# A graph kernel's count matrix laid out in DRAM with four rows of a partition side by side

## The reference

```
x_t = mlp2(x, W1n, b1n, W2n, b2n);  e_t = mlp2(edge_attr, W1e, b1e, W2e, b2e)
out = x + segment_sum(x_t[src] * e_t * dp_scale, dst) * res_w
x   = layernorm(x + layernorm(out) * gamma + beta)      # layer 1, then its norm
row, col = [src, loops], [dst, loops];  deg = segment_sum(1, col)
for _ in range(2):                                      # two hops
    h = segment_sum(deg^-1/2[row] * deg^-1/2[col] * h[col], row)
x   = layernorm(x + (h @ W.T + b))
```

## Time and profile before

| what | us |
|---|---|
| timed, median of 3 runs | 7476.43 (7473.94 to 7482.64) |
| profiled execution, its span | 9194.2 |
| own time of the profiled execution | none is given beside its span |
| stage of the profile: setup, to the first edge MLP | 0 to 180 |
| phase 1 | 180 to 6890 |
| norm | 6890 to 7001 |
| the two hops | 7001 to 9168 |
| tail | 9168 to 9194 |

### The profile page before, as it was taken

How to read it: one execution, slowest core, us unless ns; L and a number is a source line. 1 busy time by engine, 2 the same in 40 slices (tenths; PEclk the granted TensorE clock), 3 DMA queues, 4 the chain that set the end, 5 groups by cost and what they waited for, 6 DMA issues and landing times.

```text
span 9194.2 us, 153579 instructions
## 1 busy us (share of the span) xinstructions
PE 6574.3 (72%) x51112; PEld 5130.6 (56%) x51113; DVE 4933.3 (54%) x6884; ACT 4449.3 (48%) x6632; POOL 3623.7 (39%) x3315
## 2 busy tenths in 40 slices
PE   6566666666666666666666565666565899999999
PEld 3344444444444444444444444444344899989998
DVE  2455555555555555555555555555557455545555
ACT  1344444444444444444444333344333677766666
POOL 1565555655555565565444444444430000010000
PEclk9666666666666666666666666666667999999999
DMA  3233333333333333333232222223223566666665
GB/s 105 49 60 59 64 54 65 64 55 64 55 63 55 64 58 61 64 59 57 45 53 51 51 52 50 52 48 51 49 47 115 175 200 193 200 180 187 191 189 168
DMA packets 1979721, 809.87 MB, mean 88 GB/s; under 512 B 1680075, under 2 KB 1906563, under 8 KB 1978995
## 3 DMA queue, kind: packets, MB, share of 16 engines
q1 hardware_dynamic: 1845056, 677.46, 32.6%
q0 software_dynamic: 107552, 121.32, 6.2%
q10 hardware_dynamic: 27018, 9.90, 0.4%
HBM read 590.00 MB, written 218.34 MB: 88 GB/s over the span
## 4 chain that ended last, share of the span: by engine, by line
PE 50%; issue 16%; another core or an unknown queue 13%; ACT 10%; DVE 8%; DMA 1%; DVEq 1%; ACTq 1%; POOL 0%; SPq 0%; POOLq 0%
PE compared L869 11%; PE bank L944 11%; ACT arena L670 7%; PE bank L856 6%; PE compared L944 5%; PE bank L837 4%; PE sums L425 3%; PE sums L944 3%; DVE U L1215 2%; PE bank L850 2%; DVE arena L388 1%; DMA arena<-counts 1%; ACT H L661 1%; PE bank L860 1%
## 5 line engine op out<-in xcount | busy, mean ns | idle before, releaser
L573 POOL DMA_INDIRECT arena<-node_rows,arena x3125 | 3448.8, 1104 | 3205.4 <-DVE bank L1176 2112.9
L670 ACT ACTIVATE arena<-compared 98x512 uint8<-98x512 f32 x3936 | 2201.2, 597 | 2141.2 <-PE compared L869 1355.0
L869 PE MATMUL compared<-U 128*128 128x128 bf16 x15744 | 1861.4, 267 | 1718.1 <-issue 868.7
L869 PEld LDWEIGHTS compared<-U 128*128 128x128 bf16 x15744 | 1196.2, 117 | 2379.9 <-ACT arena L670 1137.2
L738 ACT ACTIVATE arena<-arena 128x1792 bf16<-128x1792 uint8 x868 | 1470.1, 1697 | 706.3 <-DMA arena<-counts 354.3
L1215 DVE TENSOR_TENSOR U<-iota_share,arena 128x1568 bf16<-128x1568 bf16 x984 | 958.6, 974 | 1075.8 <-PE compared L869 987.4
L1305 DVE CAST arena<-arena 128x1792 bf16<-128x1792 uint8 x868 | 948.5, 1094 | 1042.9 <-PE sums L944 587.0
L944 PE MATMUL bank<-arena 128*128 (+1 forms) x13440 | 1391.3, 247 | 9.4 <-issue 9.3
L1215 DVE TENSOR_TENSOR U<-iota_b,arena 128x2048 bf16<-128x2048 bf16 x984 | 1194.0, 1213 | 0.0
L944 PEld LDWEIGHTS bank<-arena 128*128 128x128 bf16 x13440 | 1138.2, 98 | 13.6 <-issue 13.0
L944 PE MATMUL compared<-arena 128*128 (+1 forms) x6720 | 1107.0, 247 | 34.1 <-DMA arena<-hop_parts,first_dst 23.5
(11 more groups left out here) (199 smaller groups left out, 4493.0 us busy)
## 6 DMA issues: line engine op xcount, KB each, us to landing
arena<-counts SPq DMA_DIRECT2D x1736, 224.0 KB
counts<-arena SPq DMA_DIRECT2D x124, 1568.0 KB, 7.2
arena<-in_edge_attr SPq DMA_DIRECT2D x125, 448.0 KB
arena<-node_rows,arena POOLq DMA_INDIRECT x3125
hop_parts<-arena ACTq DMA_DIRECT2D x14, 672.0 KB, 4.6
arena<-in_x_t SPq DMA_DIRECT2D x13, 256.0 KB, 2.6
node_rows<-H SPq DMA_DIRECT2D x1, 3136.0 KB, 16.4
edge_rows<-arena SPq DMA_DIRECT2D x1, 3125.0 KB
```

The lines of the kernel that those rows point to most:

```text
L573: e.indirect_dma_start(out=rows[:, q, k, :], out_offset=None, in_=node_rows, in_offset=bass.IndirectOffsetOnAxis(ap=src_i[:, t:t + 1], axi ...
L670: nc.scalar.activation(stage[0:B, k, v:v + VB, :].rearrange("p v n -> p (v n)"), compared[0:B, c % 2, :], ACT.Copy).then_inc(s_ev, 1)
L869: mm = nc.tensor.matmul(compared[:, c % 2, n * P:(n + 1) * P], HOH[:, j % 2, VB * c + n, :], LOH[:, j % 2, VB * c + n, :], start=True, sto ...
```

## The change

The count matrix keeps its values and its bytes. What moves is the place of each in DRAM, and with it the order in which the hop takes them.

- **Layout.** `counts` was [124·128 rows, 12,544 columns]; it is now [124·32, 98·512]. Rows 4v to 4v+3 of a block stand side by side for each node block, so that a store writes 3,136 pieces of 512 bytes in place of 12,544 of 128.
- **Hop loads.** A DRAM row now holds four count rows, and 128 DRAM rows are a whole round. A load takes all four row blocks for some of the range's 14 node blocks: `BS` = 4, 3, 4 and 3 of them. The buffers of DVE (a = 0, 2) have 2,048 bytes per partition, those of ACT (a = 1, 3) 1,536; all had 1,792.
- **Hop matmuls.** `hop_block` runs four matmuls in a row into the same half bank, one for each row block; before, successive matmuls went to successive halves. The first and last rounds go by buffer, with the same 14 zero matmuls.
- **Which row is which.** The rows of the partitions are permuted, so the tables are too: POOL makes a selection table `pick` (a memset and an affine_select of 128 by 2,048), PE applies it with 16 float32 matmuls of 62 columns behind a new wait (`s_hop_rows`), and DVE copies the two tables out of PSUM behind another (`s_picked`). Two small memsets go.
- **Gathers.** The tiles' first targets take 26 tile columns (`TC`) in place of 25, the last four of 96 rows, and their load is three DMAs, not two. Each hop has 26 gathers. The zero block's hop rows need no memset now (L1277), and the waits for the last stores stay.

```diff
+    PIECE = RING * P
+    BS = [(0, 4), (4, 7), (7, 11), (11, 14)]
-        counts = nc.dram_tensor("counts", [RB * P, COLS], u8).ap()
+        counts = nc.dram_tensor("counts", [RB * PR, B * PIECE], u8).ap()
...
             def store_block(k, q):
                 e.wait_ge(s_ev, last_use(k) + (1 + 2))
-                e.dma_start(counts[bass.ds(k * P, P), :].rearrange("v (a b) -> a v b", b=P), stage[0:B, q, :, :])\
-                    .then_inc(s_cst[q], 16)
+                e.dma_start(counts[bass.ds(k * PR, PR), :].rearrange("v (a c) -> a v c", c=PIECE),
+                            stage[0:B, q, :, :].rearrange("a (v w) n -> a v (w n)", w=RING)).then_inc(s_cst[q], 16)
...
-                        e.dma_start(raw[:, a, :, :].rearrange("p b n -> p (b n)"),
-                                    counts[bass.ds((n * RING + a) * P, P), ig * BG * P:(ig + 1) * BG * P])\
+                        b0, b1 = BS[a]
+                        row0 = (n + (a + 1)) * P - (a + 1) * P
+                        e.dma_start(raw[a], counts[bass.ds(row0, P), (ig * BG + b0) * PIECE:(ig * BG + b1) * PIECE])\
...
+            e.memset(pick, 0.0).then_inc(s_fill, 1)
...
+            e.affine_select(out=pick, in_=pick, compare_op=ALU.not_equal, fill=1.0,
+                            base=0, pattern=[[P, RING], [-1, RING], [1, P]], channel_multiplier=-RING)
...
-                for s in range(TB):
+                for s in range(TC):
...
-                        nc.scalar.activation(ring[:, a, :, :], raw[:, a, :, :], ACT.Copy).then_inc(s_conv[a], 1)
+                        nc.scalar.activation(ring[a], raw[a], ACT.Copy).then_inc(s_conv[a], 1)
...
+            e.wait_ge(s_hop_rows, 1)
+            for k in range(RING):
+                for w in range(RING):
+                    mm = nc.tensor.matmul(
+                        picked[:, k, :, :], pick[:, k, w, :],
+                        row_table[:, :, :].rearrange("p a (r w) -> p a r w", w=RING)[:, :, :, w:w + 1]
+                        .rearrange("p a r w -> p a (r w)"), start=(w == 0), stop=(w == RING - 1))
+            mm.then_inc(s_picked, 1)
...
+            def hop_block(h, ig, n, a, rows_of):
+                e.wait_ge(s_conv[a], n + (rounds_before(h, ig) + 2))
+                b0, b1 = BS[a]
+                for b in range(b0, b1):
+                    o = hop_bank[b // 2][:, b % 2 * 3 * D:(b % 2 + 1) * 3 * D]
+                    for w in range(RING):
+                        at_b = (b - b0) * PIECE + w * P
+                        mm = nc.tensor.matmul(o, ring[a][:, at_b:at_b + P], rows_of[w], start=False, stop=False)
+                mm.then_inc(s_afree[a], 1)
...
             def last_round(h, ig):
                 n = ROUNDS - 1
-                for a in (0, 1):
-                    hop_block(h, ig, n, a, hop_in[h][:, n * RING + a, :])
-                bank_by_bank(h, ig, n, (2, 3), last=True)
+                rows_of = [moving(h, n, w) for w in range(RING)]
+                for a in range(RING):
+                    hop_block(h, ig, n, a, rows_of)
+                    for j in range(BS[a][0] // 2, BS[a][1] // 2):
+                        nc.tensor.matmul(hop_bank[j][:, 0:6 * D], ones_b[0:1, :], zeros_b[:, 0:6 * D],
+                                         start=False, stop=True).then_inc(s_bank, 1)
...
-            link(nc.vector.memset(row_dst[:, FULL:RB], -1.0))
-            link(nc.vector.memset(row_tile_f[:, FULL:RB], 0.0))
...
+            e.wait_ge(s_picked, 1)
+            nc.vector.tensor_copy(row_dst[:, :].rearrange("p (r k) -> p k r", k=RING), picked[:, :, 0, :])
+            nc.vector.tensor_copy(row_tile[:, :].rearrange("p (r k) -> p k r", k=RING), picked[:, :, 1, :])\
+                .then_inc(s_rows_made, 1)
...
-            for h in range(2):
-                if h == 1:
-                    for q in range(2):
-                        e.wait_ge(s_cst[q], 16 * ((FULL + 1 - q) // 2 + 1))
-                nc.vector.memset(hop_in[h][:, FULL:RB, :], 0.0).then_inc(s_empty, 1)
+            for q in range(2):
+                e.wait_ge(s_cst[q], 16 * ((FULL + 1 - q) // 2 + 1))
...
-                nc.vector.tensor_copy(ring[:, a, :, :], raw[:, a, :, :]).then_inc(s_conv[a], 1)
+                nc.vector.tensor_copy(ring[a], raw[a]).then_inc(s_conv[a], 1)
```

More of the change, by code:

```diff
@@ L41, in gnn_two_layers @@
     COLS = B * P
+    PR = P // RING
+    LAST = P - PR
+    TC = RB - B
+    TW = TC - RING
+    assert RB == FULL + 1 and TW * P + RING * LAST >= T > TW * P + (RING - 1) * LAST
     IG = 7
@@ L44, in gnn_two_layers @@
     ROUNDS = RB // RING
-    assert RB == FULL + 1 == G - 1 and BG * IG == B and BG % 2 == 0 and BG // 2 == 7
+    assert RB == G - 1 and BG * IG == B and BG % 2 == 0 and BG // 2 == 7
     V = 16
@@ L918, in _, with moving @@
             sum_by_node(e, regs, G - 1, 0, 0, parts_2[:, 0])
-            def bank_by_bank(h, ig, n, of, first=False, last=False):
-                for a in of:
-                    e.wait_ge(s_conv[a], n + (rounds_before(h, ig) + 2))
+            def moving(h, n, w):
+                if isinstance(n, int):
+                    return hop_in[h][:, n * RING + w, :]
+                return hop_in[h][:, bass.ds(n * RING + w, 1), :].rearrange("p a f -> p (a f)")
+            def hop_block(h, ig, n, a, rows_of):
[7 more added lines that the diff above has]
+                mm.then_inc(s_afree[a], 1)
@@ L924, in bank_by_bank, with first_round @@
+            def first_round(h, ig):
                 before_it = banks_before(h, ig)
-                for j, o in enumerate(hop_bank):
-                    if first:
+                rows_of = [moving(h, 0, w) for w in range(RING)]
+                for a in range(RING):
+                    for j in range(-(-BS[a][0] // 2), -(-BS[a][1] // 2)):
                         if before_it:
                             e.wait_ge(s_taken, before_it - len(hop_bank) + j + 1)
-                        nc.tensor.matmul(o[:, 0:6 * D], ones_b[0:1, :], zeros_b[:, 0:6 * D], start=True, stop=False)
-                    for a in of:
-                        for i in range(2):
-                            mm = nc.tensor.matmul(o[:, i * 3 * D:(i + 1) * 3 * D], ring[:, a, 2 * j + i, :],
-                                                  hop_in[h][:, n * RING + a, :], start=False, stop=False)
-                        if j == len(hop_bank) - 1:
-                            mm.then_inc(s_afree[a], 1)
-                    if last:
-                        nc.tensor.matmul(o[:, 0:6 * D], ones_b[0:1, :], zeros_b[:, 0:6 * D], start=False, stop=True)\
-                            .then_inc(s_bank, 1)
@@ L940, in hop_block @@
-            def hop_block(h, ig, n, a, moving):
-                e.wait_ge(s_conv[a], n + (rounds_before(h, ig) + 2))
-                for b in range(BG):
-                    o = hop_bank[b // 2][:, b % 2 * 3 * D:(b % 2 + 1) * 3 * D]
-                    mm = nc.tensor.matmul(o, ring[:, a, b, :], moving, start=False, stop=False)
-                mm.then_inc(s_afree[a], 1)
-            def first_round(h, ig):
-                bank_by_bank(h, ig, 0, (0, 1), first=True)
-                for a in (2, 3):
-                    hop_block(h, ig, 0, a, hop_in[h][:, a, :])
+                        nc.tensor.matmul(hop_bank[j][:, 0:6 * D], ones_b[0:1, :], zeros_b[:, 0:6 * D],
+                                         start=True, stop=False)
@@ L958, in hop @@
             def hop(h, ig, first, last):
                 with e.Fori(first, last) as n:
+                    rows_of = [moving(h, n, w) for w in range(RING)]
                     for a in range(RING):
-                        hop_block(h, ig, n, a, hop_in[h][:, bass.ds(n * RING + a, 1), :].rearrange("p a f -> p (a f)"))
+                        hop_block(h, ig, n, a, rows_of)
             def first_hop_sweep(h):
```

65 lines of the change are left out of this document (40 added, 25 removed).

## The result

The changed kernel takes **7461.0 us** (median of 8 runs, 7454.8 to 7463.1) against 7476.65 for the kernel before (8 runs, 7473.9 to 7482.6): a ratio of 0.9976, 95% interval [0.9967, 0.9985], 15.6 us faster. The forecast was 7,482 us with "no change" as the likeliest case. The time lies inside the range, but a small gain that is clear of the noise was not what I forecast.

What follows compares the result with a forecast made beforehand. The prediction held phase 1 bound by POOL and PE side by side and the hops by PE alone. Small terms (2 + 0.6 − 1 − 0.3 + 2.8 + 1.3) summed to +5.4 us, giving 7,482 us, range 7,345 to 7,575.

Steps and rivals of the forecast that it cites:

- Between column ranges: Where one column range of the hops follows another: 14 zero matmuls cost 0.38 us each, nothing is late, 0.
- The store, 0 on the path: Count-block store in phase 1: 8 us or less in 512-byte pieces, but no engine waits for it, so 0.
- Four matmuls in a row into a region, 0: PE in the hops: four successive matmuls adding into the same region cost nothing extra, 0.
- rival C: Hops, slower: adding four times in a row into one region costs 2.1 ns, +51 us, so 7,533; chance 0.12.
- Conversions: Hops: DVE's conversion goes from 1.094 to 1.25 us, ACT's from 1.697 to 1.45.
- DVE being late, +2: Hops: a guessed six late loads cost DVE's longer conversions about 0.3 us more each, +2 us, bounds 0 and 95.
- Gathers, +2.8: POOL in the hops: one more gather per hop, awaited by each hop's first range, 2 × 1.39 = +2.8 us.
- Setup +1.3: Setup: 16 float32 matmuls with waits and copies take 8.6 us, mostly covered; 1.3 us charged (0 to 8.6).
- Start of the hops −1: Start of the hop: PE's first matmul needs only DVE's buffer 0, ready about 1 us earlier, −1 (0 to −1.5).
- Phase 1 is bound by POOL and PE side by side: Phase 1, timed group of 40.3 us: POOL needs 36.6 us, PE is busy 34.8, so both bind it.
- A: Phase 1, faster: timed groups wait for stores; 7,359 if one us per store counts, floor 7,023; chance 0.29.
- B: Hops, slower: DVE's buffers come late, 0.33 us at each of 289 waits for a load, +95 us, 7,577; chance 0.14.

Runs made afterwards that it cites:

- e2: The changed kernel with its zero matmuls one by one again, each next to its bank's own matmuls: 7477.75 us, ratio 0.9999 to the kernel before.
- e3: The changed kernel with the 128-byte store of the kernel before: 7461.8 us, ratio 0.9980 to the kernel before.
- e5: The kernel before with only its store changed, to 512-byte pieces: 7478.4 us, ratio 0.9999 to the kernel before.
- e9: The changed kernel without the setup's 16 float32 matmuls and their wait, tables copied unpermuted: 7461.2 us, ratio 0.9978 to the kernel before.
- e12: The changed kernel with zero matmuls of 128 contracted rows in both the hops and phase 1: 7437.1 us, ratio 0.9945 to the kernel before.
- e10: The changed kernel with the hops' zero matmuls contracting 128 rows in place of one: 7435.6 us, ratio 0.9949 to the kernel before.
- second profile: The kernel before, unchanged, profiled once more in one execution: 7480.0 us, profiled span 7478.2 us.

## Why the prediction was wrong

**The step that failed** is "Between column ranges": "each of 14 zero matmuls costs 0.38. [...] Nothing is late, 0." The 0.38 was a mean, and I carried it over as if it were a price of the matmul. It is 0.16 for the matmul and 0.21 for each switch out of and back into the real ones, and the change, by walking buffers in place of banks, cuts the switches from 13 to 7. Worth 13 × 1.3 = −17 us, measured −17.5 alone and +16.7 undone. The rows that show it were there to be read in the first trace as in the second: from a zero matmul to the next zero one 0.17 us (5639.23 to 5639.40), to the next real one 0.27 (5635.02 to 5635.29). From the first trace:

```profile
7338.24 0.33 PE L937 MATMUL compared<-zeros_b,ones_b 1*128 1x384 bf16 x1
7338.50 0.51 PE L932 MATMUL sums<-arena 128*128 128x192 bf16 x4
7338.94 0.33 PE L937 MATMUL sums<-zeros_b,ones_b 1*128 1x384 bf16 x1
7339.11 0.32 PE L929 MATMUL compared<-zeros_b,ones_b 1*128 1x384 bf16 x1
```

**The other terms.** Their sum was +5.4 and is 0.0 (e2 against before). One by one:

- The store, 0 on the path: right. Undone it costs 0.7 us (e3), done alone 0.6 (e5), both within the noise. Its own time was right too (8 us or less; it is 7).
- Four matmuls in a row into a region, 0: right. The ranges of e2 take 148.2 us, as the shortest ones of before; rival C, 2.1 ns each, would have shown as +3.6 us per range.
- Conversions, 1.25 and 1.45 us forecast: 1.227 and 1.483 measured. DVE being late, +2: it is +4.9 (waits of PE for L1305 or L1334 in range 0: 3.6 us before, 8.5 after), but ACT's greater slack, to which I gave no price, takes back 1.5 there (1.94 to 0.45) and 3.5 up to the last range, where PE waited 4.24 us for ACT and 0.22 for DVE before, and now 0.95 for DVE alone.
- Gathers, +2.8 for two hops: only hop 0 pays. Its wait for the gathered rows grew from 24.35 to 28.0 us, +3.65, more than the one instruction of 1.39, as POOL's mean rose from 1178 to 1302 ns in this pair. (Over all profiles the wait is 23.5 to 25.5 us with 25 gathers and 26.0 to 28.2 with 26.) Hop 1 has no such wait.
- Setup +1.3: 0 (e9). Start of the hops −1: the wait ahead of the first zero matmul is 2.7 us shorter, since it no longer waits for ACT's first conversion, which began after DVE's. The first real one comes 1.8 earlier: from the start of DVE's first conversion to it are 3.11 us before (5298.93 to 5302.04) and 1.28 after (5293.48 to 5294.76).
- "Phase 1 is bound by POOL and PE side by side": not so for PE's busy time. e12 takes 40 us of it away and a group stays as long.

**The rivals.** A (timed groups wait for stores) was the only road to "faster" that I gave, 0.29, and it is refuted by e3 and e5. The true road was none of my rivals, and only by chance lies inside the range. B's mechanism exists in range 0 at a twentieth of its price. Of the reasoning on the profile, one half held: the lag wasn't in the timed runs, so that a timed group had to be some 40 us (it is 37.5 with one visit and about 44 with two). The other half, that it would go with the stores, did not.

## What to carry to other kernels

A matmul that exists only to set flags should contract as many rows as its neighbours: with one row it stops the overlap of weight loads before and behind it, 0.21 us each time in the hops, 38 us of the kernel before in all (7475.7 to 7437.5). In phase 1, where PE isn't what a group waits for in the end, the same edit gave nothing. Price such a helper from two rows, one where it stands alone and one where it stands beside its like; a mean over both hides what a reordering does. And when a large change moves the time by little, look at what was rewritten in passing: the layout, the store and the loads were worth nothing, and the loop that they forced was worth all of it.

## What the runs showed of the hardware

- A weight load for one row takes 0.09 us, for 128 rows 0.10, in agreement with the Trainium skill ("TensorE: Matmul & The Clock Gate", LDWEIGHTS (loading the stationary operand)), which counts columns alone. The price of a switch to one row and back stands beside it: 0.21 us for the pair, at a granted clock of 0.99, the 2.4 GHz level.
- A load of 128 rows does start under a matmul of 128 rows (the rows of e10). The same page, The mechanism, lists that loads overlap with matmuls in flight only where their row groups differ. Here they overlap where both have 128 rows, and fail to where one has 128 and the other 1, 3, 32 or 64. Nothing here tells of counts between 64 and 128.
- One profiled execution out of 13 here took 1,718 us longer than the timed ones, with waits of up to 23.4 us for something that the trace doesn't name. Four others with the same 128-byte stores had none of it; its cause is open. A span far above the timed median calls for a second profile before any sum is made on it.
- The page's "us to landing" of the store went from 7.2 (6.9 in the second profile) to 10.2, while the windows show it in some 7 us and not 12 to 13. For this transfer the DMA share of short windows was the better witness.
